# Graph layer kernel: edges counted by pairs of tiles in 25 groups of nodes, laid among the feature products, and all score weights made on TensorE

## The reference

```python
xn = _layernorm(x, axis=-1)
x1 = relu(xn @ W_ah + b_ah)
def gat_conv(x, src, dst, W, a_src, a_dst, b):      # three layers, 4 heads of 192 each
    h = (x @ W).reshape(N, H, C)
    as_n = (h * a_src).sum(-1)
    ad_n = (h * a_dst).sum(-1)
    e = leaky_relu(as_n[src] + ad_n[dst], 0.2)
    m = segment_max(e, dst); p = exp(e - m[dst]); s = segment_sum(p, dst)
    return segment_sum((p / s[dst])[:, :, None] * h[src], dst) + b
```

## Time and profile before

| | |
|---|---|
| median of 3 runs | 1414.38 us (1414.12 to 1414.83) |
| span of the profiled execution | 1412.8 us |
| that execution's time around its span | not listed; the runs' median is 1.6 us above the span |
| PE busy | 1354.6 us, 96% |
| DVE busy | 1041.0 us, 74% |
| ACT busy | 505.5 us, 36% |
| POOL busy | 45.6 us, 3% |
| mean granted clock of TensorE | 0.988 |

### The profile page before, as it was taken

How to read it: one execution, slowest core, us unless ns; L and a number is a source line. 1 busy time by engine, 2 the same in 40 slices (tenths; PEclk the granted TensorE clock), 3 DMA queues, 4 the chain that set the end, 5 groups by cost and what they waited for, 6 DMA issues and landing times.

```text
span 1412.8 us, 21085 instructions
## 1 busy us (share of the span) xinstructions
PE 1354.6 (96%) x8144; PEld 1259.9 (89%) x8144; DVE 1041.0 (74%) x1927; ACT 505.5 (36%) x824; POOL 45.6 (3%) x49
## 2 busy tenths in 40 slices
PE   5999999999999899999999999999999999999896
PEld 5854666999999799999999999999999999999884
DVE  7838987899999742686776677676767766768667
ACT  5211244334443511444333432343243334333373
POOL 5000000000000050000000000000000000000000
PEclk9999999999999899999999999999999999999998
DMA  9410001122221675511101110110012011104003
GB/s 270 155 40 2 0 1 33 56 89 89 74 86 37 196 212 168 121 37 37 39 1 71 37 40 1 71 43 34 13 58 76 1 70 37 42 1 143 1 1 110
DMA packets 23621, 91.60 MB, mean 65 GB/s; under 512 B 3681, under 2 KB 4864, under 8 KB 20589
## 3 DMA queue, kind: packets, MB, share of 16 engines
q1 hardware_dynamic: 22609, 88.07, 19.4%
q10 hardware_dynamic: 924, 2.30, 0.6%
HBM read 79.30 MB, written 11.06 MB: 64 GB/s over the span
## 4 chain that ended last, share of the span: by engine, by line
PE 53%; DVE 7%; ACT 1%; issue 0%; DVEq 0%
PE psum L1704 25%; PE psum L102 8%; PE psum L103 8%; PE psum L104 8%; DVE hN L1328 1%; PE psum L1718 1%; DVE prob L1312 1%; DVE prob L1306 1%; PE psum L1758 1%; DVE acc L1445 0%; DVE acc L1350 0%; DVE x1l L1335 0%; PE psum L1773 0%; ACT prob L1534 0%; DVE acc L1366 0%
## 5 line engine op out<-in xcount | busy, mean ns | idle before, releaser
L1704 PE MATMUL psum<-hN,prob 125*125 125x193 f32 x2400 | 409.0, 327 | 1.5 <-DVE hN L1328 1.5
L1704 PEld LDWEIGHTS psum<-hN,prob 125*125 125x125 f32 x2400 | 395.3, 187 | 2.0 <-issue 1.8
L1534 ACT ACTIVATE prob<-prob,acol 125x1250 f32<-125x1250 f32 x120 | 160.9, 1341 | 381.4 <-DVE prob L1306 381.4
L1312 DVE SCALAR_TENSOR_TENSOR prob<-prob,cnt 125x1250 f32<-125x1250 f32 x120 | 174.6, 1455 | 56.4 <-ACT prob L1534 56.4
L1306 DVE SCALAR_TENSOR_TENSOR prob<-vrow,ncol,urow 125x1250 f32<-125x1250 f32 x120 | 181.8, 1515 | 9.5 <-PE psum L1704 9.5
L747 DVE CUSTOM_DVE_ANT_0 junk<-mask,arow 125x1250 bf16<-125x1250 uint8 x120 | 174.8, 1457 | 3.1
L102 PE MATMUL psum<-woh,xlh 128*125 128x384 f32 x360 | 128.3, 357 | 2.6 <-DVE acc L1350 2.6
L103 PE MATMUL psum<-wol,xlh 128*125 128x384 f32 x360 | 123.5, 343 | 0.0
L102 PE MATMUL psum<-wph,x1h 128*125 128x384 f32 x330 | 118.4, 359 | 4.8 <-PEq L963 1.9
L104 PE MATMUL psum<-woh,xll 128*125 128x384 f32 x360 | 122.8, 341 | 0.0
L103 PE MATMUL psum<-wpl,x1h 128*125 128x384 f32 x330 | 111.9, 339 | 0.0
(11 more groups left out here) (242 smaller groups left out, 2214.5 us busy)
## 6 DMA issues: line engine op xcount, KB each, us to landing
arow<-scratch_a SPq DMA_DIRECT2D x12, 625.0 KB, 4.0
urow<-scratch_uv SPq DMA_DIRECT2D x12, 625.0 KB, 4.2
vrow<-scratch_uv SPq DMA_DIRECT2D x12, 625.0 KB, 5.7
wq_raw<-in_w_qkv SPq DMA_DIRECT2D x6, 1152.0 KB, 6.7
wp_raw<-in_w_pair SPq DMA_DIRECT2D x6, 1152.0 KB, 7.7
wo_raw<-in_w_out SPq DMA_DIRECT2D x6, 1152.0 KB, 5.1
wl<-in_w_gat SPq DMA_DIRECT2D x4, 1152.0 KB, 10.4
xN<-in_x SPq DMA_DIRECT2D x10, 336.0 KB
```

What stands on the lines that cost most here:

```text
L1312: nc.vector.scalar_tensor_tensor(prob[n % RING][:, :], prob[n % RING][:, :], 1.0, cnt[:, n % NT, :], op0=ALU.min, op1=ALU.mult).then_inc(p ...
L1534: nc.scalar.activation(prob[n % RING][:, :], prob[n % RING][:, :], ACT.Exp, bias=acol[:, n // NT, n % NT:n % NT + 1]).then_inc(e_ready, 1)
L1704: last = nc.tensor.matmul(bank(t // 2)[0:P, 193 * (t % 2):193 * (t % 2) + 193], ring[:, t * P:(t + 1) * P], hN[i % 2][:, j, 193 * s:193 * ...
```

## The change

- **Windows.** 25 windows of WD = 50 nodes in place of ten of 125. A source node is split into its tile t (0 to 9) and its place within it: `part_f` and `tile_f`, found on VectorE by ten comparisons and sums of 160 columns. A unit is counted by `hot_part` (125 columns: place of the source) and `hot_pair` (500 columns: 50 nodes d by ten tiles t), and one matmul of 500 columns adds it to one bank, so the table comes out with the source on the partitions, as `cnt` wants it.
- **Turns.** ScalarE copies a window to `cnt` and, as zero or one in bf16, to `has`; TensorE turns `has` by matmuls with a unit matrix once a whole tile of 125 nodes is there, ten matmuls for each of ten tiles (MASKED_AT), and ScalarE copies them to `mask`. `ct` and its transposes go.
- **Buffers.** CE is 2 in place of 3.
- **Place.** Windows 0 to 9 stand in TensorE's queue behind `hidden(8)` to `hidden(17)`, one behind each; windows 10 to 24 behind the scores. Each window loads its two registers at its start, on both engines.
- **Score weights.** All three layers by `score_weights` and `turn_score_weights` on TensorE, behind products 7, 9, 13 and 8, 10, 14 (counted from zero). VectorE's 96 sums and their loads (`w_gat`, `a_gat`) go; `w_turned` has three layers in halves of 384 columns, loaded into four places.

The core of the diff:

```diff
-CE = 3
+CE = 2
+WD = 50
+NW = N // WD
+WN = WD * NT
...
-        REACHED = 11
-        TURNED = 13
-        TURNS = ((6, 0, 4), (7, 4, 4), (6, 8, 2))
+        LAYER_AT, TURNED_AT = {7: 0, 9: 1, 13: 2}, {8: 0, 10: 1, 14: 2}
+        FIRST = 8
+        EARLY = len(X1) - FIRST
+        MASKED_AT = {8: 0, 9: 1, 10: 2, 11: 3, 13: 4, 15: 5, 18: 6, 20: 7, 23: 8, 24: 9}
+        LOW_AT, SHIFT_AT, WQ_AT = 11, 13, 16
+        TURNS = ((2, 0, 4), (3, 4, 4), (7, 8, 2))
...
-            for w in range(NT):
-                with dve.Fori(*reached[w], CE) as unit:
+            for w in range(NW):
+                first = dve.value_load(g["reach_row"][0:1, 2 * w:2 * w + 1], min_val=0, max_val=ET - 1)
+                end = dve.value_load(g["reach_row"][0:1, 2 * w + 1:2 * w + 2], min_val=1, max_val=ET)
+                with dve.Fori(first, end, CE) as unit:
                     for e in range(CE):
                         dve.reg_add(units, units, 1)
                         dve.wait_ge(hot_free, dve.snap(units))
-                        nc.vector.tensor_scalar(hot_dst[:, e, 0:P], node_id[:, w * P:(w + 1) * P],
-                                                dst_f[:, bass.ds(unit + e, 1)], None, ALU.is_equal)\
-                            .then_inc(hot_ready, 1)
-                        nc.vector.tensor_scalar(hot_src[:, e, :], node_id[:, :], src_f[:, bass.ds(unit + e, 1)],
-                                                None, ALU.is_equal).then_inc(hot_ready, 1)
+                        nc.vector.tensor_scalar(hot_part[:, e, 0:P], place[:, 0:P], part_f[:, bass.ds(unit + e, 1)], None,
+                                                ALU.is_equal).then_inc(hot_ready, 1)
+                        nc.vector.tensor_scalar(hot_pair[:, e, :], place[:, :], float(WN * w), pair_f[:, bass.ds(unit + e, 1)],
+                                                ALU.add, ALU.is_equal).then_inc(hot_ready, 1)
+                if w == LOW_AT:
+                    dve.wait_ge(at_ready, len(CH))
...
+            def window(w):
+                if w == 0:
                     pe.wait_ge(reach_in, 16)
...
+                else:
+                    pe.wait_ge(ct_ready, 2 * (w - 1))
+                first = pe.value_load(g["reach_row"][0:1, 2 * w:2 * w + 1], min_val=0, max_val=ET - 1)
+                end = pe.value_load(g["reach_row"][0:1, 2 * w + 1:2 * w + 2], min_val=1, max_val=ET)
...
+                with pe.Fori(first, end, CE):
+                    for e in range(CE):
+                        pe.reg_add(units, units, 2)
+                        pe.wait_ge(hot_ready, pe.snap(units))
+                        nc.tensor.matmul(here, hot_part[:, e, 0:P], hot_pair[:, e, :], start=False, stop=False,
+                                         skip_group_check=True).then_inc(hot_free, 1)
...
+                if i in LAYER_AT:
+                    score_weights(LAYER_AT[i])
+                if i in TURNED_AT:
+                    turn_score_weights(TURNED_AT[i])
+                if i == len(X1) - 1:
+                    scores()
+                if i >= FIRST:
+                    window(i - FIRST)
+                    if i - FIRST in MASKED_AT:
+                        turn_mask(MASKED_AT[i - FIRST])
+            turn_scores()
+            for w in range(EARLY, NW):
+                window(w)
+                if w in MASKED_AT:
+                    turn_mask(MASKED_AT[w])
```

More of the change, by code:

```diff
@@ L411, in _ @@
-            dve.wait_ge(xt_full, 2 * NT)
+            own.done(nc.vector.tensor_scalar(tile_f[:, :], src_f[:, :], float(P), None, ALU.is_ge))
+            for j in range(2, NT):
+                own.done(nc.vector.scalar_tensor_tensor(tile_f[:, :], src_f[:, :], float(P * j), tile_f[:, :],
+                                                        op0=ALU.is_ge, op1=ALU.add))
+            own.done(nc.vector.scalar_tensor_tensor(part_f[:, :], tile_f[:, :], -float(P), src_f[:, :], op0=ALU.mult, op1=ALU.add))
@@ L564, in _, with score_weights @@
-            pe.wait_ge(const_ready, 5)
+            def score_weights(layer):
+                pe.wait_ge(wT_in, 32 * (layer + 1))
+                if layer == 0:
+                    pe.wait_ge(blk_in, 16)
+                    pe.wait_ge(xl_ready, 2 * NT)
+                else:
+                    pe.wait_ge(waT_ready, 2 * layer)
+                for half in range(2):
+                    q = 2 * layer + half
+                    for c in range(KT):
+                        last = nc.tensor.matmul(bank(2 + half)[0:2 * HL, 0:384], a_blk[:, layer, c, :], wT[q if q < 4 else q - 2][:, c, :],
+                                                start=c == 0, stop=c == KT - 1)
+                last.then_inc(waT_full, 1)
@@ new lines, in turn_score_weights @@
+            def turn_score_weights(layer):
+                pe.wait_ge(waT_ready, 2 * (layer + 1))
+                if layer:
+                    pe.wait_ge(wa_ready, layer)
+                for k in range(KT):
+                    last = nc.tensor.transpose(bank(7)[:, 2 * HL * k:2 * HL * (k + 1)], waT[:, 128 * k:128 * (k + 1)],
+                                               ident[0:2 * HL, 0:2 * HL])
+                last.then_inc(wa_full, 1)
+            units = pe.alloc_register("pe_units")
@@ new lines, in turn_mask @@
+            def turn_mask(t):
+                pe.wait_ge(ct_ready, 2 * -(-P * (t + 1) // WD))
+                for k, (at_bank, t0, n) in enumerate(TURNS):
+                    if t:
+                        pe.wait_ge(turn_free, len(TURNS) * (t - 1) + k + 1)
+                    elif k < 2:
+                        pe.wait_ge(waT_ready, 2 * LAYERS)
+                    else:
+                        pe.wait_ge(wa_ready, LAYERS)
+                    if t == 2 and k == 2:
+                        pe.wait_ge(ab_taken, 1)
+                    for j in range(n):
+                        last = nc.tensor.matmul(bank(at_bank)[0:P, P * j:P * (j + 1)],
+                                                has[t // 2 % 2][:, t0 + j, P * (t % 2):P * (t % 2 + 1)], eye[:, 0:P],
+                                                start=True, stop=True)
+                    last.then_inc(turn_full, 1)
@@ new lines, in scores, with turn_scores @@
+            def scores():
+                pe.wait_ge(x1_free, len(X1))
+                pe.wait_ge(wa_ready, LAYERS)
+                for i, (c0, n) in enumerate(CH):
+                    for k in range(KT):
+                        last = nc.tensor.matmul(bank(4 + i)[0:2 * HEADS, 0:n], wa[:, k, :], x1T[:, k, c0:c0 + n],
+                                                start=k == 0, stop=k == KT - 1)
+                    last.then_inc(at_full, 1)
+            def turn_scores():
+                pe.wait_ge(at_ready, len(CH))
+                pe.wait_ge(turn_free, 2 * len(TURNS))
+                for t in range(NT):
+                    last = nc.tensor.transpose(bank(7)[0:P, t * 2 * HEADS:(t + 1) * 2 * HEADS], abT[:, t * P:(t + 1) * P],
+                                               ident[0:2 * HEADS, 0:2 * HEADS])
+                last.then_inc(ab_full, 1)
```

326 lines of the change are left out of this document (121 added, 205 removed).

## The result

The changed kernel takes 1460.56 us, the median of 4 runs (1456.34 to 1464.41), beside 1414.25 us for the kernel before (1412.0 to 1414.83): a ratio of 1.033, 95% interval 1.0308 to 1.0352. The profiled execution has a span of 1457.4 us (before 1412.8) and a mean granted clock of 0.951 (before 0.988). The forecast was 1460, in the range 1434 to 1486. The attention's first matmul starts at 286.72 us instead of 241.86, so the whole difference arises in this stage.

What follows compares the result with a forecast made beforehand. TensorE's serial queue through products and counting was taken as the bound, a pass set by the two-buffer round trip. Span 1412.8 plus 18.2 and 10.5 gave 1441.5, median 1443.1; clock 12 and 5 gave 1460, range 1434 to 1486.

Steps and rivals of the forecast that it cites:

- Score weights, +18.2: Feature products: two more layers on TensorE, 16.9 us, plus 1.3 for the scores' later turn; VectorE's dropped sums worth nothing.
- The pass, 1.14 us: Counting loop: two units cost the way round one buffer, 1.14 us, 0.57 each against 0.62 before; VectorE's work hides.
- Windows 0 to 9, 66.7 us at full clock: Among products: 48 passes of 1.14 us, 54.7, plus about 1.2 us a window; register loads cost nothing.
- Windows 10 to 24, 67.5 us at full clock: Behind scores: 40 passes, 45.6; window changes 16.5; mask turns 3.6; window 11's minimum over the scores 1.8.
- The clock, 12 in the loops and 5 in the products: TensorE's clock drops: half of up to 24.5 us in loops, 5 of up to ten times 2.9 us in products.
- The tail, 5.1 us: From the last window's closing matmul to the next stage: left at the old kernel's 5.1 us.
- The sum: Whole kernel: +18.2 and +10.5 on the span, 1.6 to the median, 17 for the clock, giving 1460 us.
- What was said to show it: Trace signs: passes 1.1 to 1.4 us apart, TensorE idle over 40 us, 0.33 us halves, attention at 263 to 295 us.
- full clock (1443): Rival: clock full throughout, 1443 us, or 1433 with a way round a tenth shorter; chance 0.2.
- Clock low in all loops and after them (1497): Rival: TensorE at the low clock in every loop and following products, 1497 us; chance 0.17.
- VectorE's own pace (1400): Rival: waits overlap, a pass costs 0.84 us and the loads run ahead, 1400 us; chance 0.06.

Runs made afterwards that it cites:

- experiment 3: Changed kernel with score weights made on TensorE for the first layer only and used for all three: 1442.48 us.
- experiment 8: On top of experiment 7, layer 0's score weights back on VectorE, six windows among the products, 19 windows' loads ahead: 1402.82 us.
- experiment 1: Changed kernel with three buffers in place of two, 69 passes of three units: 1427.24 us.
- experiment 4: Changed kernel with fill: TensorE multiplies 384 columns of zeros after each unit, counts unchanged: 1443.88 us.
- experiment 5: Changed kernel with all 25 windows behind the scores, none among the products: 1473.55 us.
- experiment 6: Changed kernel with late windows' register loads made ahead and spread, in TensorE's product chunks and before VectorE's windows 0, 1, 3, 5, 7: 1443.47 us.
- The first attempt: Changed kernel with registers of windows 10 to 24 loaded ahead all in one place, VectorE before window 10, TensorE beside the scores: 1461.15 us.
- experiment 7: Changed kernel with three buffers and the spread register loads together: 1416.67 us.

## Why the prediction was right

- **Score weights, +18.2.** Right: 7.91 and 0.54 us again in the trace, and experiment 3 gives 18 for the 16.9. For the later turn of the scores the forecast had 1.3: it waits 1.8 us instead of 0.6. That the sums' departure from VectorE is worth nothing fits experiment 8, where one layer given back to it goes with a gain.
- **The pass, 1.14 us.** Right: 1.15, and 0.25 more at the low clock, 1.40, as forecast. That it is the round trip and not VectorE's work is confirmed by experiment 1, where the waits go and VectorE's own 0.43 us a unit (0.42 in the prediction) comes out. Between its pass and VectorE's pace the prediction had 26.4 us; the third buffer gave 33, with 11 more units to pay for, since most of the clock's price goes too (7.2 us in the products alone).
- **Windows 0 to 9, 66.7 us at full clock.** 66.5 us in the run with fill. The loads do hide there: TensorE starts those of window 1 at 90.0 us, beside the score weights' matmuls, and opens it at 95.91; experiment 5, which takes the cover away, loses 13 us.
- **Windows 10 to 24, 67.5 us at full clock.** 68.5 us in the run with fill. The window change is 1.95 us instead of 1.9, and the loads' 15 x 1.1 = 16.5 us show as 16.3 us in 14 changes in experiment 6. Its whole gain, 15 us (by the ratios) to 17 us (by the medians), meets 16.5 only because 5 us of clock and a price of 4.7 us elsewhere cancel. The first attempt at it failed because its own plan put 30 loads on an engine that others were waiting for.
- **The clock, 12 in the loops and 5 in the products, 17 together.** Experiment 4 gives 17 together; the split is off. The nine products among the windows lost 7 us (46.0 against 38.8 with fill, from the first matmul to the one behind), the loops about 9 (4 in windows 0 to 9, 5 behind them). Half of a range was a choice and not a mechanism, so the clock's term was partly luck. "The clock may come back" was half right: it comes back between windows that lie among products, where TensorE works through, and hardly behind the scores (0.59 over 77.5 us).
- **The tail, 5.1 us.** 3.8: the last window has one bank of 500 columns to copy and ten short turns (1.33 us), where the prediction took over the old tail unchanged.
- **The sum.** 1460 against 1460.56 is closer than its terms. The tail is 1.3 us under its forecast, the clock's term about 1 us by the trace, and the late windows 1 us over; that these nearly cancel is luck. Apart from the two parts of the clock, each term is met to within about a microsecond, and the mechanism is the forecast one.
- **What was said to show it.** All but one: "72 matmul halves of score weights at 0.33 us" is the distance from one to the next; the duration in their rows is 0.49 us, because they overlap.

Of the rivals, full clock (1443) is what experiment 4 makes true by fill. Clock low in all loops and after them (1497) is out: of the passes that lie wholly at one level without a product in between, 30 are at the low and 25 at the full clock. VectorE's own pace (1400) needs the third buffer and hidden loads; with both, experiment 7 comes to 1416.7. That rival left out the turn of the loop (1.48 - 3 x 0.43 = 0.19 us a pass, 13 us for 69) and the 11 more units of passes of three (5 us). With the 5.5 us that the spread loads cost in the products this is more than the 16.7 us, so this account is an estimate that does not close.

## What to carry to other kernels

When a unit gets smaller, count the way round one buffer, not each engine's work: with two buffers the pass here was 1.15 us for 0.86 us of VectorE's work, and it moved with TensorE's clock; one more buffer cured both. Register loads among other work were free here only while the queue held enough ahead of them (a pair behind three matmuls left a gap of 0.39 us, one behind twelve none), so put them where it does, in small groups. And moving an idle engine's work onto the engine whose time is the stage's time costs its full length, however small it looks.

## What the runs showed that was not expected

- **The low clock holds on at a busy TensorE.** Behind the scores the clock does not swing evenly but stays at 1.2 GHz for long stretches in which PE's rows cover four fifths of the time, since the slow matmuls fill more of each pass; it returns to 2.4 GHz for short ones:

```profile
209.00:232.60 23.60, 19.50 (x68) 10.06 (x67) 12.05 (x48) 6.85 (x15) 0.93 (x2) 0.50 0.00 0
232.80:239.40 6.60, 4.03 (x13) 1.54 (x12) 4.30 (x19) 3.52 (x7) 0.00 (x0) 1.00 0.08 12
239.80:259.90 20.10, 16.27 (x52) 7.92 (x51) 10.62 (x44) 8.74 (x15) 0.00 (x0) 0.50 0.00 0
```

  In window 0, with no change of window in it, the loop alone brings the clock to 0.63. Behind the scores the kernel with spread loads runs the same loop of two buffers at 0.99: so in the changed kernel the pauses at the window changes, 1.4 us of VectorE's each, go with the low clock there. What in window 0 does it without them is not shown. The Trainium skill, "TensorE: Matmul & The Clock Gate", section "A second HAM failure mode: psum-queue depth-cycling", has short idling between groups of matmuls make the clock swing between its levels. The trace agrees that it changes level without any long pause, five times from 205.70 to 283.20 us; here it stays at the low level for 20 to 27 us at a time and at the full one for 3 to 7, so the mean is 0.59.
- **Adding useless matmuls made the kernel quicker**, by 17 us with 196 x 384 columns. They run in the time in which TensorE waits for the next hot_pair.
- **A wait's releaser misled.** VectorE's 1.43 us before each late window is put down to "PE psum L589"; with the registers loaded ahead (experiment 6) the same change takes 0.72 us from the last hot_part to the next window's first (241.14 to 241.86) instead of 1.95, with the matmul where it was.
